# A decoder layer whose attention half runs from a written list: the same 741 steps in another order

## What is computed

```python
x = layernorm(x + attn(x, Wq, bq, Wk, bk, Wv, bv, Wo, bo))       # 4 x 512 x 256, 16 heads of 16, causal
x = layernorm(x + xattn(x, ctx_768, w_q, w_k, w_v, w_out, b_out)) # 64 context rows per batch, 16 heads of 64
x = layernorm(x + moe(x, Wg, W1, b1, W2, b2))                     # top 2 of 8 experts, 256 -> 1024 -> 256
```

## Time and profile before

| | us |
|---|---|
| median of 3 executions (746.45 to 747.99) | 747.08 |
| the profiled execution's own time | 746.32 |
| its span, first to last instruction | 744.6 |
| attention half, by the first instruction of the expert half | 448.4 |
| first maxima of batch 0, PE | 47.4 |
| transpose of batch 0's maxima (`mT:0:0`) | 94.7 |
| first maxima of batch 2 and of batch 3, PE | 182.4 and 267.1 |
| DVE busy, share of the span | 74% |
| PE busy, share of the span | 80% |

### The profile page before, as it was taken

The page is one execution under the profiler, slowest core; times in us unless marked ns, Lnnn a source line. Parts: engine busy times, 40 slices in busy tenths (PEclk is TensorE's granted clock), DMA queues, the critical chain, the costliest instruction groups (busy, mean ns, idle before and its releaser), DMA issues. The chain is left out here.

```text
span 744.6 us, 13174 instructions
## 1 busy us (share of the span) xinstructions
...
## 2 busy tenths in 40 slices
PE   3795778986899969888996751589999999999950
...
PEclk9796587998899989999998995579999999999975
...
GB/s 234 200 54 100 98 59 143 137 191 215 25 1 1 112 173 1 58 4 84 1 2 114 1 0 118 240 199 267 249 284 282 260 276 282 255 291 177 76 246 113
DMA packets 74381, 104.64 MB, mean 141 GB/s; under 512 B 5184, under 2 KB 62216, under 8 KB 73296
## 3 DMA queue, kind: packets, MB, share of 16 engines
...
## 5 line engine op out<-in xcount | busy, mean ns | idle before, releaser
L235 DVE TENSOR_REDUCE rowmax<-M 128x1 f32<-128x384 f32 (+3 forms) x176 | 104.8, 637 | 52.3 <-PE M L225 51.2
L208 PE MATMUL HB<-xT,w 128*128 128x256 f16 (+1 forms) x1104 | 110.4, 262 | 6.2 <-DVE xT L1528 6.2
L1292 POOL DMA_INDIRECT scratch_ys<-y,dst x39 | 75.6, 1940 | 84.8 <-DVE y L1543 79.3
L653 ACT ACTIVATE probs<-R 128x1024 f32<-128x1024 f32 x80 | 80.7, 1027 | 56.2 <-PE R L963 56.0
L208 PEld LDWEIGHTS HB<-xT,w 128*128 128x128 f16 x1104 | 96.0, 100 | 18.9 <-DVE xT L1528 8.3
L1669 PE MATMUL YB<-w,h 128*128 128x256 f16 x936 | 105.8, 273 | 0.0
L1373 ACT ACTIVATE hf<-HB,b 128x256 f32<-128x256 f32 (+1 forms) x184 | 71.2, 438 | 57.3 <-PE HB L208 56.4
L1669 PEld LDWEIGHTS YB<-w,h 128*128 128x128 f16 x936 | 91.5, 98 | 10.4
L524 POOL TENSOR_SCALAR_AFFINE_SELECT probs<-probs 128x256 f32<-128x256 f32 x128 | 49.5, 408 | 104.8 <-ACT probs L653 104.4
L220 PE MATMUL M<-ks,qs 48*128 48x128 f16 (+3 forms) x256 | 39.0, 344 | 37.8 <-DVE rowmax L235 23.3
L1555 DVE SCALAR_TENSOR_TENSOR h<-hf,h 128x512 f16<-128x512 f32 (+1 forms) x92 | 56.8, 618 | 3.2
...
...
## 6 DMA issues: line engine op xcount, KB each, us to landing
...
```

What stands on the lines that cost most here:

```text
L208: last = nc.tensor.matmul(out, left(a, k), right(b, k), start=(k == 0 and m == 0), stop=(k == n - 1 and m == 2))
L235: return nc.vector.tensor_reduce(rowmax[:, t, par * PAIRS + p0:par * PAIRS + p0 + pairs], bank[:, 0:pairs * wide].rearrange("p (n w) -> p ...
L653: A.activation(probs[:, n % RING, :, :], bank[:, :, :], ACT.Exp, scale=1.0 / (QS * QS)).then_inc(empty, 1)
L1292: pool.indirect_dma_start(out=dram["ys"], in_=y[:, n % 2, t, :], in_offset=None, out_offset=bass.IndirectOffsetOnAxis(dst[:, at:at + 1], 0 ...
```

## The change

Only the text of `ORDER` changes. It holds the same 741 steps; 52 stand more than ten places from where they stood. Below stand its beginning, down to the first fold steps, and three later places.

```diff
-wh:0:0 wh:0:1 xT:0:0 xT.l:0:0 xT:0:1 wh:1:0 xT.l:0:1 q:0:0 x_in:1:0 cT:0:0 wh:1:1 cT.l:0:0 ql:0:0 cT:1:0 wk:0:0 q:0:1
-ql:0:1 cT.l:1:0 v:0:0 xT:1:0 xT.l:1:0 wk.l:0:0 store:0:0 wk:1:0 wk.l:1:0 W:0:0 xT:1:1 wk:2:0 stack:0:0 W.l:0:0 W:1:0
-xT.l:1:1 wk.l:2:0 q:1:0 va:0:0 wg:0:0 W.l:1:0 ql:1:0 kv:0:0 q:1:1 ql:1:1 kv.l:0:0 v:1:0 m:0:0 kv:1:0 m:0:1 kv.l:1:0
-m:0:2 va:1:0 kv:2:0 wo:0:0 m:0:3 m:0:4 kv.l:2:0 m:0:5 A:0:0 A.l:0:0 m:0:6 m:0:7 m:0:8 m:0:9 m:0:10 m:0:11 m:0:12
-m:0:13 m:0:14 m:0:15 m:0:16 A.s:0:0 store:1:0 m:0:17 wo.l:0:0 m:0:18 kv:3:0 m:0:19 m:0:20 m:0:21 stack:1:0 mT:0:0
-x_in:2:0 kv.l:3:0 max:0:0 m:1:0 VW:0:0 VW.l:0:0 VW.s:0:0 A:1:0 m:1:1 A.l:1:0 s:0:0 s:0:1 wg.l:0:0 m:1:2 s:0:2 xT:2:0
+xT:0:0 wh:0:0 xT.l:0:0 wh:0:1 xT:0:1 wh:1:0 xT.l:0:1 wh:1:1 q:0:0 ql:0:0 x_in:1:0 wk:0:0 cT:0:0 cT.l:0:0 q:0:1 v:0:0
+ql:0:1 wk.l:0:0 wk:1:0 xT:1:0 xT.l:1:0 store:0:0 wk.l:1:0 xT:1:1 xT.l:1:1 stack:0:0 W:0:0 cT:1:0 W.l:0:0 W:1:0 wk:2:0
+wk.l:2:0 cT.l:1:0 va:0:0 kv:0:0 W.l:1:0 q:1:0 kv.l:0:0 kv:1:0 wo:0:0 wo.l:0:0 ql:1:0 q:1:1 kv.l:1:0 v:1:0 m:0:0 m:0:1
+m:0:2 A:0:0 ql:1:1 m:0:3 m:0:4 m:0:5 kv:2:0 va:1:0 m:0:6 x_in:2:0 m:0:7 m:0:8 m:0:9 m:0:10 kv.l:2:0 m:0:11 m:0:12
+m:0:13 m:0:14 m:0:15 store:1:0 A.l:0:0 stack:1:0 m:0:16 m:0:17 m:0:18 kv:3:0 m:0:19 m:0:20 m:0:21 kv.l:3:0 A.s:0:0
+mT:0:0 max:0:0 VW:0:0 xr_in:0:0 VW.l:0:0 VW.s:0:0 A:1:0 wg:0:0 A.l:1:0 xT:2:0 xT.l:2:0 m:1:0 A.s:1:0 s:0:0 VW:1:0
...
-w:0:7 w:0:8 s:0:15 m:1:20 VW:6:0 VW.l:6:0 VW.s:6:0 pv:0:2 s:0:16 m:1:21 ql:2:1 ct:0:2 store:2:0 s:0:17 A:7:0 v:2:0
-mT:1:0 A.l:7:0 max:1:0 s:0:18 A.s:7:0 VW:7:0 w:0:9 s:0:19 xb:0:0 w:0:10 VW.l:7:0 s:1:0 ct.n:0:2 w:0:11 pv:0:3 s:1:1
+w:0:9 ct.n:0:2 A:7:0 A.l:7:0 mT:1:0 w:0:10 max:1:0 A.s:7:0 VW:7:0 s:0:19 w:0:11 pv:0:3 ct:0:3 VW.l:7:0 VW.s:7:0 s:1:0
...
-stack:2:0 w:1:1 o.d:0:1 r:0:1 s:1:5 n:0:0 s:1:6 m:2:0 s:1:7 n:0:1 x1b:0:0 m:2:1 xa:0:0 vw:0:0 ax:0:0 xa.l:0:0 m:2:2
+n:0:0 n:0:1 s:1:3 x1b:0:0 vw:0:0 v:2:0 m:2:0 m:2:1 xa:0:0 xa.l:0:0 m:2:2 xa:0:1 s:1:4 s:1:5 xa.l:0:1 m:2:3 va:2:0
...
-r:0:2 s:1:18 m:2:19 xs:0:3 s:1:19 O:0:2 m:2:20 w:1:10 xp:0:3 w:1:11 O.d:0:2 m:2:21 store:3:0 pv:1:3 T:0:6 T.l:0:6
-T:0:7 ct:1:3 T.l:0:7 ct.n:1:3 mT:2:0 cx:1:0 cx.l:1:0 cx:1:1 cx.l:1:1 n:0:2 O:0:3 O.d:0:3 r:0:3 n:0:3 max:2:0 s:2:0
+ct.n:1:3 mT:2:0 T:0:6 T.l:0:6 T:0:7 T.l:0:7 cx:1:0 O:0:3 cx.l:1:0 O.d:0:3 cx:1:1 r:0:3 cx.l:1:1 n:0:3 max:2:0
...
```

68 lines of the change are left out of this document (37 added, 31 removed).

## The result

| | before | after |
|---|---|---|
| median of 4 executions, us | 747.07 (746.45 to 747.99) | 761.70 (759.09 to 764.37) |
| ratio | | 1.0187, 95% interval 1.0147 to 1.0227 |
| the profiled execution, and its span | 746.32, 744.6 | 762.77, 761.0 |

The change is slower, as forecast, but by 14.6 us where I had 5.4.

What follows compares the result with a forecast made beforehand. The prediction took the attention half to be a chain of PE work with waits in it. Its terms, +9.9 + 1.1 - 2.0 - 2.0 - 1.3 = +5.7 us on 746.32, gave 752.0, forecast as 752.5, range 745.8 to 758.5.

Steps and rivals of the forecast that it cites:

- Step 1: Up to the first maxima: later `kv:0` and a new wait before `v:1:0` delay `m:0:0` by 9.9 us, bounds +9.0 and +13.6.
- the second rival: The clock falls in the new waits, with `v:1:0` and part of `kv:0` at half clock: 756.7 us, chance 0.22.
- Step 2: Batch 0's 22 maxima, `m:0:0` to `mT:0:0`: +1.1 us, bounds -1.7 and +1.3; moving `wo.l` out saves nothing.
- Step 3: Stacks asked for sooner: nothing gained or lost for `stack:1`; -1.2 us at `stack:3`.
- Step 4: The fold, `mT:0` to `VW:7`: waits at `VW:2` go and steps move out, -2.0 us, bounds -4 and +0.5.
- Step 5: Batch 2's maxima to `m:3:0`: moved steps cost 2.2, idle time gives back 3.0; -2.0 us, bounds -4 and +1.
- Step 6: The last batch: `O:3:1` and `O:3:2` wait less, `w:3:2` and `s:3:6` give 0.5; -1.3 us, bounds -3 and +1.
- The rival in which the later stages take back more: From `mT:0` to `m:3:0` over 11.0 us come back, making the change faster: 742.8 us, chance 0.13.

Runs made afterwards that it cites:

- after_headfill2: The changed kernel with unread matmuls added, 18 ahead of `W:1`, 16 ahead of `kv:0`'s first wait and 14 ahead of `v:1:0`; 755.3 us.
- wo_alone: The kernel before with only `wo:0:0` and `wo.l:0:0` moved ahead of `kv.l:1:0`; 747.7 us, ratio 1.0045.
- old_fold: The changed kernel with the old order put back between `max:0:0` and `m:2:0`; 761.1 us, ratio 1.0205.
- after_wo: The changed kernel with `wo:0:0` back behind `kv:2:0` and `wo.l:0:0` back behind `m:0:17`; 754.9 us, ratio 1.0127.

## Why the forecast failed: the size of step 1, and steps 4 and 6

- **Step 1, the step that failed first: +9.9 forecast, +13.6 measured.** The mechanism held: `kv:0` first (36.3 forecast, 37.06), then `v:1:0` behind `wo.l` with a wait of 3.7 (3.68), `m:0:0` behind both. The mis-sized term is the clock in this stretch. `kv:0` 6.1 us instead of the 5.6 that I gave it, `q:1:0` 4.2 instead of 2.8, `v:1:0` 4.1 instead of 2.8, and `kv:0` 0.8 late since `W:1` ran at half too: 4.0 together, against a surplus of 3.7. I had this as the upper bound, +13.6 to the tenth, and as the second rival. The sum had a slip as well: 48.2 and 6.6 and 2.8 make 57.6 and not 57.3. I had read in the earlier trace rows that `q:1:0` ran slow behind a wait, and then let a similar wait of 3.7 us before `v:1:0` pass at the full clock. after_headfill2 shows the cause: 6.4 us come back when PE is kept at work. That is more than the surplus, since I had counted part of the half clock of `kv:0`.
- **Step 2: +1.1 forecast, -0.8 measured.** `m:0:0` to `m:0:6` took 13.6 us on DVE (16.3 before) where I had 15.4: the clock was still full up to 69.9, so the six maxima with `A:0` took 8.8 us instead of my 10.5, and `kv:2` then 5.5. `kv.l:2` at +2.0 is right (`m:0:6` to `m:0:19` 27.3 against 25.3), and so is `wo.l` at nothing (wo_alone).
- **Step 3: right.** `stack:1`'s last DMA landed at 76.45 and `m:1:0` came over 30 us later.
- **Step 4: -2.0 forecast, +0.2 and then +1.5 more measured.** PE's busy time fell by 1.9 us. The moves (`v:2:0` out, `w:0:9` and `w:0:10` in) account for 0.7 of it, as I had; the rest goes with the better clock, 0.93 for 0.88. The wait at `VW:2` went as I said, but the other gaps grew by 3.6 us: I had counted the wait that goes and given the new pairs 0.4. And 1.5 us were lost from `VW:7` to `m:2:0`: the steps put there were to stand in the shade of the stack's landing, and with 2.70 us for `probs` and 1.68 for `ctxT` they outgrew it. Against the same beginning, the new fold is 4.8 us longer than the old (old_fold), since the old one too got faster at the better clock (0.95 against 0.88 before). So the comparison with the trace of before flattered it.
- **Step 5: right in the sum, in part by luck.** -2.0 forecast, -2.1 measured, `m:2:0` to `m:3:0` 84.7 to 82.6. But the wait for the stack at its end gave back 3.0 us (5.97 to 2.95) where I had 1.2, and the rest of the stretch cost 0.9 where I had it give 0.8. At `m:2:0`, where I expected a wait of some 7 us, there was none.
- **Step 6: -1.3 forecast, +3.0 measured.** `O:3:0` to `O:3:1` fell by 0.8 as I said, and to `O:3:2` by another 0.8; `O:3:2` to `O:3:3` rose by 0.8, as `T:3:6` now waits for `xp:3:3`. That net -0.7 is the -0.8 of the forecast. But two terms that I had at nothing cost 3.8 us. `O:3:0` comes 2.1 us later after `m:3:0` (156.3 for 154.2): PE waits 2.98 us for `xp:3:0` at `T:3:0` where it waited 1.82, and then `S:3:4` and `S:3:5`, 12 matmuls, run at half clock, +1.7. (A wait of 1.59 us before `S:3:2` is gone in return.) And `O:3:3` runs at half clock, +1.7. The 0.5 of `w:3:2` and `s:3:6` does not show: `S:3:0` comes 139.7 us after `m:3:0` in both. The kernel before (`T:3:0`, `S:3:4`, `O:3:3`) and the kernel after:

```profile
417.82 1.10 PE L1019 MATMUL M<-ident,e_x 128*128 128x128 f32 x8 [1.82 <-POOL e_x L559]
418.76 2.75 PE L208 MATMUL M<-a_x,x1T 128*128 128x512 f16 x12
...
441.85 2.78 PE L208 MATMUL M<-vw,pT 128*128 128x256 f16 x24 [1.62 <-DVE pT L692]
```

```profile
430.60 1.09 PE L1019 MATMUL M<-ident,e_x 128*128 128x128 f32 x8 [2.98 <-POOL e_x L559]
431.52 4.44 PE L208 MATMUL M<-a_x,x1T 128*128 128x512 f16 x12
...
455.58 4.45 PE L208 MATMUL M<-vw,pT 128*128 128x256 f16 x24 [1.62 <-DVE pT L692]
```

  The slow `S:3:4` and `S:3:5` belong to the new order: they take 3.8 to 4.4 us in all thirteen traces with the new end and 2.75 in all six with the old. The slow `O:3:3` shows in six of the thirteen, and in three of the other six traces `O:3:1` or `O:3:2` is as slow (4.1 to 4.3 us), so that 1.7 is partly the luck of this trace. Moving `lg:5:0` does change who gets which M bank (`T:3:0` now takes that of `S:3:2` and not of `S:3:1`), but no run moves it alone, so which of the moved steps brings the half clock stays open.
- The expert half, carried along: 297.5 us for 296.5, +1.0.
- **Sum** in the profiled executions: 13.6 - 0.8 + 0.2 + 1.5 - 2.1 + 3.0 + 1.0 = +16.4. Of the rivals, the clock in the new waits was right, but it too counted on 5.3 us of recovery behind `mT:0`, where 2.6 were lost in the attention half. The rival in which the later stages take back more failed: it wanted over 11 us from `mT:0` to `m:3:0`, and 0.5 came.
- On "TensorE: Matmul & The Clock Gate" (the Trainium skill, Part 1), which I had weighed: its rule that full speed must be earned by activity was the better guide than my chain of full-clock durations. The number beside it is 4.09 us for `v:1:0` behind the wait and 2.78 in after_wo without it. But the earlier trace rows does not show the half clock behind each hollow, as I had it: the clock's digit is 5 in slice 5, and 8 in slices 10 and 15, where the hollows are shorter than a slice of 18.6 us.
